# Cross attention and mixture of experts in four layers: when the routing of batches 0 and 1 is issued in attentions 2 and 3

## The reference

```python
x = x + L2_xattn(layernorm(x), ctx); x = x + L2_ffn(layernorm(x))
x = x + L3_xattn(layernorm(x), ctx); x = x + L3_ffn(layernorm(x))

def xattn(x, ctx):                 # 16 heads of 64
    q, k, v = x @ w_q, ctx @ w_k, ctx @ w_v
    return softmax(q @ k.T / 8) @ v @ w_o

def ffn(x):                        # 8 experts, each token to its best 2
    top_vals, top_idx = top_k(x @ w_router, 2)
    w = softmax(top_vals)
    return sum(w[:, e] * act(x @ w1[e]) @ w2[e] for e in top_idx)
```

## Time and profile before

| | before |
|---|---|
| median of 3 runs | 1169.45 us (1161.92 to 1171.49) |
| span of the profiled execution | 1219.8 us (the page gives no other time of it) |
| PE busy | 1054.1 us, 86% |
| DVE busy | 717.3 us, 59% |
| ACT busy | 643.9 us, 53% |
| POOL busy | 571.5 us, 47% |
| steps 13 and 14 of attention 2 | 10.80 and 12.66 us |
| 64 scatters (L903) | 61.8 us, 965 ns each |

### The profile page before, as it was taken

One profiled execution on the slowest core, in us unless ns is written; L12 is line 12 of the kernel. 1 busy time (PEld: TensorE's weight loads), 2 busy tenths in 40 slices (PEclk: granted clock), 3 DMA queues, 4 the chain that ended last, 5 costly groups with the idle time before them and its releaser, 6 DMA issues.

```text
span 1219.8 us, 22199 instructions
## 1 busy us (share of the span) xinstructions
PE 1054.1 (86%) x6815; PEld 797.4 (65%) x6815; DVE 717.3 (59%) x2444; ACT 643.9 (53%) x2117; POOL 571.5 (47%) x926
## 2 busy tenths in 40 slices
PE   4988999758889998979999987777799999977994
PEld 3865788735555667856767665566566776654994
DVE  5575354476776771386767784322876776852444
ACT  2244323357778723358778862222387888731321
POOL 5223655451000152566555656366375555655452
PEclk9987999989999988889999997697899999986997
DMA  2003556599600124110000001364300000014665
GB/s 63 13 27 112 161 165 208 163 156 385 237 1 1 36 68 137 54 30 19 1 19 19 1 5 43 85 187 121 87 19 1 2 1 1 2 33 129 200 208 173
DMA packets 116005, 102.87 MB, mean 84 GB/s; under 512 B 18027, under 2 KB 97571, under 8 KB 115888
## 3 DMA queue, kind: packets, MB, share of 16 engines
q1 hardware_dynamic: 105280, 82.71, 23.3%
q0 software_dynamic: 8448, 17.20, 4.2%
q10 hardware_dynamic: 2160, 1.53, 0.5%
HBM read 65.04 MB, written 36.36 MB: 83 GB/s over the span
## 4 chain that ended last, share of the span: by engine, by line
PE 61%; DVE 16%; issue 6%; ACT 5%; POOL 4%; DMA 4%; another core or an unknown queue 3%; SPq 2%; DVEq 0%; ACTq 0%; POOLq 0%
PE ps L2973 4%; PE ps L2777 4%; PE ps L2869 4%; PE ps L2882 4%; PE ps L2779 4%; PE ps L2778 4%; PE ps L2987 3%; PE ps L3515 3%; PE ps L3519 3%; PE ps L3168 2%; PE ps L3528 2%; PE ps L3001 2%; PE ps L3327 2%; ACT ex L1323 2%
## 5 line engine op out<-in xcount | busy, mean ns | idle before, releaser
L1323 ACT ACTIVATE ex<-ps,nmx 128x154 f32<-128x154 f32 x512 | 194.0, 391 | 75.0 <-DVE nmx L2278 73.2
L1085 POOL TENSOR_TENSOR pp<-ex,rc 128x256 f32<-128x256 f32 x256 | 157.6, 615 | 146.0 <-DVE rc L2283 145.0
L2278 DVE TENSOR_REDUCE nmx<-ps 128x2 f32<-128x308 f32 x256 | 119.6, 470 | 60.2 <-PE ps L2779 59.2
L922 POOL DMA_INDIRECT yq_d<-yq,ids_q x78 | 74.7, 957 | 79.4 <-DVE yq L2030 60.6
L2973 PEld LDWEIGHTS ps<-ident,pp 128*128 128x128 f32 x640 | 73.9, 142 | 55.5 <-POOL pp L1086 46.5
L2777 PE MATMUL ps<-kp,q_s 128*128 128x308 f32 x256 | 95.5, 373 | 15.1 <-ACT ex L1323 12.6
L1323 ACT ACTIVATION_READ_ACCUMULATOR ex<-ps,nmx 128x1 f32 x512 | 105.2, 205 | 0.0
L2973 PE MATMUL ps<-ident,pp 128*128 128x128 f32 x640 | 100.1, 280 | 2.8 <-POOL pp L1086 2.8
L1440 ACT ACTIVATE pe<-ps,nmx 128x154 f32<-128x154 f32 x256 | 84.9, 394 | 32.0 <-DVE nmx L2161 30.9
L892 POOL TENSOR_TENSOR ln_r<-ln_v,mhalf 128x4 f32<-128x4 f32 x32 | 32.7, 1021 | 105.4 <-DVE ln_v L1736 86.8
L2869 PE MATMUL ps<-xc_q,w_q 128*128 128x256 f32 (+1 forms) x276 | 63.6, 371 | 19.3 <-issue 11.5
(11 more groups left out here) (481 smaller groups left out, 2831.6 us busy)
## 6 DMA issues: line engine op xcount, KB each, us to landing
w_r<-in_L_ffn_W SPq DMA_DIRECT2D x69, 256.0 KB
xq_d<-blankq SPq DMA_DIRECT2D x4, 4160.0 KB, 23.8
w_q<-in_L_ffn_W SPq DMA_DIRECT2D x46, 256.0 KB
w_q<-in_L_ffn_w SPq DMA_DIRECT2D x46, 128.0 KB
xq<-xq_d SPq DMA_DIRECT2D x24, 130.0 KB
w_s<-in_L_ffn_W SPq DMA_DIRECT2D x8, 256.0 KB
w_e<-in_L_ffn_W SPq DMA_DIRECT2D x8, 256.0 KB, 5.2
acc<-yq_d SPq DMA_DIRECT2D x8, 256.0 KB, 4.6
```

The source lines that it names most:

```text
L922: pool.indirect_dma_start(yq_d[:, :], bass.IndirectOffsetOnAxis(ap=ids_q[:, c:c + 1], axis=0), yq[k % NY][:, h, :], None).then_inc(q_out[k ...
L1085: pool.tensor_tensor(pp[st % 2][:, m % 4, 2 * j:2 * j + 2, :], w[:, :, 0:P], r.broadcast_to([P, 2, P]), ALU.mult)
L1323: ins = act.activation(ex[:, tt % NEX, j, :], ps[:, tt % 3, j * SK:(j + 1) * SK], ACT.Exp, bias=nmx8[:, tt % 8, j:j + 1], accum_out=sm8[:, ...
L2278: dve.tensor_reduce(nmx8[:, tt % 8, :], ps[:, tt % 3, 0:2 * SK].rearrange("p (h s) -> p h s", h=2), AX.X, ALU.max, negate=True).then_inc(n ...
```

## The change

The order of the routing of batches 0 and 1 changes on every engine. Batch 0's tail_sum goes on PE to the end of step 12, batch 1's tail_sum and batch 0's tail_xT to the end of step 13, and so on: everything to do with batches 0 and 1 comes about one step earlier, and in step 15 POOL issues three of batch 0's scatters. Behind step 15 the order becomes ranks(1) first, tail_shift(2) ahead of low_out(15), scale(2) ahead of high_out(15). The ring's lists follow. Lines of the new file are 1 to 3 higher than those of the old: DVE 3, PE and ACT 2, POOL's L892 and L903 1. The diff:

```diff
--- before.py
+++ after.py
@@ -76,13 +76,14 @@
 
     ORDER = [(g, b) for g in range(2) for b in range(B)] + [(2, 0), (2, 1), (3, 0), (3, 1), (2, 2), (3, 2), (2, 3), (3, 3)]
     LAST = [max(st for st in range(NST) if ORDER[st][1] == b) for b in range(B)]
-    BEHIND = {(0, "A"): [("x", 1)], (0, "C"): [("x", 2)], (2, "A"): [("x", 3)], (13, "A"): [("f", 0)], (14, "A"): [("f", 1)], (14, "D"): [("t", 0)], (15, "A"): [("lg", 0)], (15, "D"): [("t", 1)]}
+    EARLY = 3
+    BEHIND = {(0, "A"): [("x", 1)], (0, "C"): [("x", 2)], (2, "A"): [("x", 3)], (12, "D"): [("f", 0)], (13, "D"): [("f", 1), ("t", 0)], (14, "A"): [("lg", 0)], (14, "D"): [("t", 1), ("rk", 0)], (15, "A"): [("lg", 1)]}
 
     FIRST1 = {1: [0], 2: [1], 3: [2, 3]}
     BEHIND1 = {(14, "D"): [("u", 0)], (15, "A"): [("f", 0)], (15, "D"): [("u", 1)]}
     TAIL = [("f", 1), ("t", 0), ("pt", NST - 1, 3), ("o", NST - 2), ("pt", NST - 1, 1), ("pt", NST - 1, 2), ("u", 2), ("pt", NST - 1, 4), ("f", 2), ("t", 1), ("t", 2), ("o", NST - 1), ("u", 3), ("f", 3), ("t", 3)]
     NEXT = [("next", 0, i) for i in range(PREPS)]
-    ENDING = [None, None] + [[("pt", NST - 1, 1), ("rk", 0), ("pt", NST - 1, 4), ("pt", NST - 1, 3), ("f", 2), ("lg", 1), ("y", NST - 2), ("pt", NST - 1, 2), ("rk", 1), ("t", 2), ("y", NST - 1), ("lg", 2), ("f", 3)]
+    ENDING = [None, None] + [[("pt", NST - 1, 1), ("rk", 1), ("pt", NST - 1, 4), ("pt", NST - 1, 3), ("f", 2), ("y", NST - 2), ("pt", NST - 1, 2), ("t", 2), ("y", NST - 1), ("lg", 2), ("f", 3)]
                              + NEXT[0:1] * (l == 2) + [("rk", 2), ("t", 3), ("lg", 3)] + NEXT[1:2] * (l == 2) + [("rk", 3)] + NEXT[2:] * (l == 2) for l in (2, 3)]
 
     def ring(l):
@@ -904,14 +905,13 @@
 
             def region(l):
 
+                for i in range(EARLY, 2 * TB):
+                    scatter_rows(l, 0, i)
                 for i in range(2 * TB):
-                    scatter_rows(l, 0, i)
+                    scatter_rows(l, 1, i)
                     if i == 1:
                         rstd(2 * l + 1, 2)
-                for i in range(2 * TB):
-                    scatter_rows(l, 1, i)
-                    if i == 2:
-                        rstd(2 * l + 1, 3)
+                rstd(2 * l + 1, 3)
                 for b in (2, 3):
                     for i in range(2 * TB):
                         scatter_rows(l, b, i)
@@ -1146,10 +1146,12 @@
                             low_x(3)
                         elif (st, m) == (4, 0):
                             row_ids()
-                        elif (st, m) == (13, 7):
+                        elif (st, m) == (13, 3):
                             rstd(2 * l + 1, 0)
-                        elif (st, m) == (14, 7):
+                        elif (st, m) == (14, 3):
                             rstd(2 * l + 1, 1)
+                        elif st == NST - 1 and m % 2 and m // 2 < EARLY:
+                            scatter_rows(l, 0, m // 2)
                     if st % B == 1 and st < NST - B:
                         if st >= 2:
                             pool.wait_ge(*full(l, ("y", st - 2)))
@@ -1378,24 +1380,25 @@
                     if st == 0:
                         turned_x(2)
                     exps(st, 6)
-                    if st == 15:
+                    if st == 14:
                         scale(l, 1)
+                        shares(l, 0)
                     step_prep(st, 3)
                     exps(st, 7)
                     high_out(st - 1, 0)
-                    if st >= 14:
-                        tail_xT(l, st - 14)
+                    if st in (13, 14):
+                        tail_xT(l, st - 13)
                     copy_pt(st, 0)
+                    if st == 14:
+                        second_rows(l, 0)
                 high_out(NST - 2, 1)
-                shares(l, 0)
+                shares(l, 1)
                 copy_pt(NST - 1, 4)
-                second_rows(l, 0)
+                second_rows(l, 1)
                 copy_pt(NST - 1, 2)
-                shares(l, 1)
+                scale(l, 2)
                 high_out(NST - 1, 0)
                 high_out(NST - 1, 1)
-                scale(l, 2)
-                second_rows(l, 1)
                 tail_xT(l, 2)
                 second_rows(l, 2)
                 shares(l, 2)
@@ -2367,6 +2370,10 @@
                 for st in range(NST):
                     maxima(st, 0)
                     low_out(st - 2, 0)
+                    if st in (13, 14):
+                        tail_sum(l, st - 13)
+                    elif st == 15:
+                        ranks(l, 0)
                     copy_pt(st - 1, 1)
                     if st == 1:
                         variances(3)
@@ -2380,23 +2387,26 @@
                     if st == 0:
                         normed_half(2, 1)
                     elif st in (13, 14):
-                        tail_sum(l, st - 13)
-                    elif st == 15:
-                        tail_shift(l, 1)
-                        best(l, 0)
+                        tail_statistics(l, st - 13)
+                    if st >= 14:
+                        best(l, st - 14)
                     maxima(st, 3)
                     copy_pt(st - 1, 3)
-                    if st == 14:
-                        tail_scale(l, 0)
-                    elif st == 15:
-                        indices(l, 0)
+                    if st >= 14:
+                        indices(l, st - 14)
                     maxima(st, 4)
+                    if st >= 14:
+                        marks(l, st - 14)
                     if st == 0:
                         summed_up(3)
                     elif st == 1:
                         normed_half(3, 0)
                     maxima(st, 5)
+                    if st == 14:
+                        tail_shift(l, 1)
                     add_up(st - 2)
+                    if st == 13:
+                        tail_scale(l, 0)
                     if st == 0:
                         moments_half(3, 0)
                     elif st == 1:
@@ -2407,28 +2417,20 @@
                     step_prep(st, 2)
                     if st == 0:
                         moments_half(3, 1)
-                    elif st in (13, 14):
-                        tail_statistics(l, st - 13)
-                    elif st == 15:
-                        marks(l, 0)
                     maxima(st, 7)
                     step_prep(st, 3)
                 maxima(NST, 0)
                 copy_pt(NST - 1, 1)
                 low_out(NST - 2, 0)
                 low_out(NST - 2, 1)
-                ranks(l, 0)
+                ranks(l, 1)
                 copy_pt(NST - 1, 3)
                 tail_sum(l, 2)
-                best(l, 1)
                 tail_statistics(l, 2)
-                indices(l, 1)
-                marks(l, 1)
+                add_up(NST - 2)
                 tail_shift(l, 2)
-                add_up(NST - 2)
                 low_out(NST - 1, 0)
                 low_out(NST - 1, 1)
-                ranks(l, 1)
                 add_up(NST - 1)
                 best(l, 2)
                 tail_sum(l, 3)
@@ -3041,10 +3043,8 @@
                         turned_x(1)
                     elif st == 2:
                         turned_x(3)
-                    elif st in (13, 14):
-                        tail_sum(l, st - 13, *summed(l, st - 13))
-                    elif st == 15:
-                        logits(l, 0)
+                    elif st >= 14:
+                        logits(l, st - 14)
                     scores(st, 2)
                     transposes(st - 1, 2)
                     scores(st, 3)
@@ -3062,22 +3062,24 @@
                     scores(st, 7)
                     values(st - 1, 1)
                     rest_values(st - 1)
-                    if st >= 14:
-                        tail_xT(l, st - 14)
+                    if st in (12, 13):
+                        tail_sum(l, st - 12, *summed(l, st - 12))
+                    if st in (13, 14):
+                        tail_xT(l, st - 13)
+                    if st == 14:
+                        rank(l, 0)
                     transposes(st, 0)
                 st = NST - 1
                 transposes(st, 1)
-                rank(l, 0)
+                rank(l, 1)
                 transposes(st, 4)
                 transposes(st, 3)
                 tail_sum(l, 2, *summed(l, 2))
-                logits(l, 1)
                 values(st, 0)
                 project(st - 1)
                 transposes(st, 2)
                 values(st, 1)
                 rest_values(st)
-                rank(l, 1)
                 tail_xT(l, 2)
                 project(st)
                 logits(l, 2)
```

## The result

| | before | changed |
|---|---|---|
| median | 1170.47 us (4 runs, 1161.92 to 1171.99) | 1191.68 us (4 runs, 1188.36 to 1195.05) |
| ratio, with its 95% interval | | 1.0204 [1.0167, 1.0240] |
| span of the profiled execution | 1219.8 us | 1187.7 us (its run: 1189.57) |

The kernel is slower by 21 us, as forecast: 1191, and +21. The spans say the opposite of the times, and only because the profile of before came from an execution 50 us longer than its runs. Where stretches of some length are compared, it is the second.

What follows compares the result with a forecast made beforehand. The prediction took PE, DVE and ACT going round in one loop as the bound, with batch 3's routing ending the attention. Terms of 10.6 and 11.4 gave +22 us on 1219.8, scaled by 0.96 to +21: 1191, range 1174 to 1206.

Steps and rivals of the forecast that it cites:

- step 12: PE's tail_sum(0) now at the end of step 12 delays the next matmul: +0.4 us per attention.
- step 13: Bank wait for DVE's tail_sum(0), statistics before maxima 3, and tail_xT(0) at its end: +1.9 us per attention.
- step 14: Bank wait, DVE's work between maxima and PE's 2.4 us gap for scale(1): 18.5 us long, +5.8 and +6.3.
- step 15 to project(15): From step 15's start, late rstd(2) holds tail_shift(2), scale(2), high_out and low_out; project(15) at 29.0 us: +2.5 and +2.8.
- project(15) to the experts: Behind project(15) nothing changes its order, and POOL's idle 3.92 and 4.20 us cover four late scatters: 0.
- rival (c): Clock falls in new gaps before project(15) and in step 14: +28 to +36 us, 1196 to 1204; chance 0.15.
- PE's wait for the bank: Start of step 14: transposes(13, 1) waits for DVE's tail_sum(1), maxima 1 at 3.7 us instead of 2.2.
- rstd(2) behind seven scatters: On POOL behind step 15: rstd(2) follows seven scatters instead of two, starting at 23.9 us, done at 24.9.
- The 1.8 us per attention: Step 15's three early scatters might each last longer by up to one DVE copy; the forecast would be 1194.
- (a): Not slower: steps' idle time absorbs the moved work, project(15) 2 to 4.5 us earlier; 1161 to 1166; chance 0.08.
- (b): Mild: step terms mostly absorbed or the wait for rstd(2) hidden, +4 to +11 us, 1173 to 1181; chance 0.16.
- (d): Batch 0's first scatter in step 15 finds ranks(0) unwritten and holds POOL's normalises; 1178 to 1194; chance 0.02.

Runs made afterwards that it cites:

- the second profile: The kernel before, unchanged, run and profiled again: 1168.77 us, ratio 0.9999, span 1166.6 us.
- the kernel with rstd(2) back: The changed kernel with rstd(2) behind two scatters behind step 15, as in the kernel before, not behind seven: 1189.08 us, ratio 1.0179 to the kernel before.
- both rstd back: The changed kernel with rstd(2) behind two scatters and rstd(3) behind three scatters of batch 1, as in the kernel before: 1184.59 us, ratio 1.0133.
- the kernel with the extra statistics: The kernel before with eight further statistics of 128 columns on DVE ahead of maxima 3 of step 12: one run, 1169.44 us.
- the kernel without early scatters: The changed kernel with both rstd back and no scatter inside step 15, all eight of batch 0 behind it: 1183.29 us, ratio 1.0143 to the kernel before.
- tail_sum first: The changed kernel with DVE's tail_sum of batches 0 and 1 ahead of the first maxima of steps 13 and 14: 1192.32 us, ratio 1.0195.

## Why the prediction was right

The time was met to 1 us, and the sum term by term against the second profile (attention 2, attention 3):

| term | forecast | measured |
|---|---|---|
| step 12 | +0.4, +0.4 | +0.43, +0.42 |
| step 13 | +1.9, +1.9 | +1.99, +1.98 |
| step 14 | +5.8, +6.3 | +6.62, +8.88 |
| step 15 to project(15) | +2.5, +2.8 | +2.4, +2.4 |
| project(15) to the experts | 0, 0 | +0.4, -1.5 |

- Steps 12 and 13 were right to 0.1 us.
- Step 14 was mis-sized. Maxima by maxima the hand count was good: maxima 3 to 6 of attention 2 came at 7.75, 9.67, 11.39 and 13.23, forecast 7.8, 9.7, 11.3 and 12.9. What it lacked was the clock, which I had put into rival (c). In attention 3 the mean granted clock of step 14 was 0.81, in attention 2 0.97: behind the idle 1.95 us at its start logits took 1.60 us where attention 2, behind 2.21 us, took 0.95. At a clock of 1.00 the same instructions took 18.58 us, as in attention 3 of the kernel with rstd(2) back; the forecast has 18.5. (Its last sum, 15.9 + 0.46 + 1.14 + 0.4 + 0.7, is 18.6.) Over the four kernels that issue the same in step 14 it goes from 18.58 to 21.01. Windows over step 14, of the changed kernel in both attentions and of that one in attention 3:

```profile
689.24:708.51 19.27, 13.75 (x90) 10.28 (x91) 12.18 (x54) 13.11 (x49) 8.28 (x19) 0.97 0.01 2
...
1015.14:1036.15 21.01, 16.71 (x90) 12.46 (x91) 12.24 (x53) 12.86 (x47) 8.03 (x19) 0.81 0.01 2
...
1015.98:1034.56 18.58, 13.34 (x90) 9.90 (x91) 12.09 (x53) 12.47 (x46) 8.01 (x19) 1.00 0.01 2
```

- PE's wait for the bank, forecast as 1.5 us at maxima 1, was right: without it PE comes to tail_xT(1) 1.3 to 1.5 us sooner. Taken away alone it left step 14 at 19.4 us all the same, because the clock fell behind the wait for scale(1).
- rstd(2) behind seven scatters, and through it tail_shift(2), scale(2), high_out and low_out, was right: rstd(2) was forecast at 23.9 and came at 24.0, and with both rstd back in place the time is 7 us less. What I had not seen is that rstd(3) had been moved in the same way; "nothing changes its order" behind project(15) was wrong.
- The 0 behind project(15) rested on POOL's idle 3.92 and 4.20 us of the first profile, which the second does not have. That the term came out near 0 is luck. Its +0.4 is no more than what equal instructions vary by: the kernel with the extra statistics took 34.8 us from project(15) to the experts in attention 2, the second profile of before 32.5.
- "What ends the attention is batch 3's routing, not the number of scatters" was wrong for attention 3. I had read it from the disturbed profile's idle 4.20 us. In the second profile POOL's scatters run without a gap there from rstd(3) on, and the chain of waits of attention 3 goes through them (start, us, what):

```profile
1060.74 0.96 POOL xq_d L903
...
1063.27 4.55 DMA xq_d<-xe,slot_q
...
1069.14 2.40 DMA xq<-xq_d
...
1071.59 0.44 PE ps L2857 x2
```

In the changed kernel the chain has scatters ahead of rstd(2), but from project(15) on it goes through DVE's and PE's routing of batch 3 to the experts, with no scatter:

```profile
1086.42 1.83 PE ps L2850 x8
...
1088.25 6.00 PE ps L2754 x16
...
1094.24 0.23 PE ps L2859 x2
```

So the early scatters may be worth something there, the 1.5 us in the table: the changed kernel takes its 29.8 us at a clock of 0.69, before its 31.2 at 0.78, so the clock is not what shortens it. It is not shown by itself: with both rstd back it is 29.5 us with the early scatters and 31.3 without, but at clocks of 0.88 and 0.78. In attention 2 neither chain has a scatter between project(15) and the experts. The size was small enough not to move the forecast.
- The three early scatters took 1.06, 1.02 and 1.01 us in attention 2, against 0.965 in the mean of before. The 1.8 us per attention from which the forecast would have been 1194 did not show in them.
- The sum of 22 was scaled by 0.96 for the long first profile. The steps are equally long in both profiles, so it should not have been: unscaled, 22 on the 1169.45 known then is 1191.5, on 1170.47 it is 1192.5. That the sum and the time agree so well is partly luck: the terms are 24 us in the traces, some of them by the clock, and 3 us of the difference between the two spans lie in stretches that the change does not touch.

Rivals (a) and (b) fell, since none of steps 12 to 14 came out shorter than forecast. Of (c) a part came: the slow step 14 above, and project(15) of attention 2, whose six rows last 0.76 to 0.63 us in the changed kernel and 0.48 to 0.39 in the second profile of before; the time stayed below its 1196. (d) fell, as the first scatter starts 5.3 us into step 15, behind ranks(0).

## What to carry to other kernels

Work that is taken out of a tail and put into a loop that goes round three engines costs there what the loop can't absorb: half of DVE's added time in the one load that was priced, plus every wait that then stands last. Ask of an engine's list not only what an instruction costs but what is queued behind it: a small rstd behind seven scatters held up DVE, ACT and PE. And when the largest of several waits goes and nothing changes, don't conclude that it was covered: follow the step row by row to where the saved time is lost again. Here that was a stretch at a lower clock behind a later wait, and with that wait cut short as well the saving showed.

## What the runs showed of the hardware

- Two profiles of one kernel had spans of 1219.8 and 1166.6 us; the attention steps were equal to 0.01 us, and the difference lay around the routing's tail, the transfers and the experts. A profiled span should be held against its own run's time before stretches of it are compared.
- The granted clock fell in stretches of some executions and not of others with the same instructions. Step 14 took from 18.58 us at 1.00 to 21.01 at 0.81 in the four kernels that issue the same there. Step 15 of attention 2 up to maxima 7 took 11.33 us at 0.97 with both rstd back and 14.22 at 0.68 in the kernel without early scatters, whose PE issues the same there; with tail_sum first it took 14.31 at 0.67, and with the same order of step 15 in the changed kernel 11.37 at 0.90.
- Behind PE's wait for scale(1) at the end of step 14 the clock was below 1.00 (0.50 to 0.91) in nine of the ten stretches where the wait was 1.88 us, in five kernels, and 1.00 in five of the six where it was 0.53 us or less, in three. The Trainium skill, page "TensorE: Matmul & The Clock Gate", section "HAM oscillation — how this bites in real kernels", describes such falls behind waits between groups of matmuls. These rows agree in kind. But a wait alone does not decide it: at the start of step 14 of the changed kernel 1.95 us in attention 3 were followed by slow logits (1.60 us), and 2.21 us in attention 2 by fast ones (0.95).
